# A macaron block on one core: scores of two groups in one burst, one bank for both FFNs' sums, queries and keys in one step

## The reference, cut to what matters

```python
def ffn(x):                                    # quantised weights, hidden width 2048
    gate, up = split(x @ ternary_quant(w_gate_up).T)
    return rms_norm(silu(gate) * up) @ ternary_quant(w_proj).T

def attention(x):                              # 32 heads of 16, blocks of 128 tokens
    q, k, v = x @ Wq.T, x @ Wk.T, x @ Wv.T
    # each block of 128 queries sees its own 128 keys and the 128 before them
    # (dist = query - key must lie in 0..128), none before the sequence's start
    probs = softmax(where(valid, q @ k.T / 4, lowest))
    return (probs @ v) @ Wo.T

x = x + 0.5 * ffn(layernorm(x))        # A
x = x + attention(layernorm(x))        # B
x = x + 0.5 * ffn(layernorm(x))        # C
```

## Time and profile before

| | us |
|---|---|
| three runs | 2028.21, 2030.60, 2031.13 |
| median | 2030.6 |
| the profiled execution | 2030.56 |
| its span, first to last instruction | 2028.7 |
| busy: TensorE matmul | 1919.7 |
| busy: VectorE | 1541.2 |
| busy: ScalarE | 1493.1 |

### The profile page before, as it was taken

How to read it: one execution, slowest core, us unless ns; L and a number is a source line. 1 busy time by engine, 2 the same in 40 slices (tenths; PEclk the granted TensorE clock), 3 DMA queues, 4 the chain that set the end, 5 groups by cost and what they waited for, 6 DMA issues and landing times. The chain is left out here.

```text
span 2028.7 us, 37471 instructions
## 1 busy us (share of the span) xinstructions
PE 1919.7 (95%) x12447; PEld 898.9 (44%) x12688; DVE 1541.2 (76%) x4079; ACT 1493.1 (74%) x2871; POOL 510.9 (25%) x559
## 2 busy tenths in 40 slices
PE   6678899999999999999999999999999999999887
PEld 3353344444444444444444444444444444444332
DVE  8966788777876888777777888777786788777673
ACT  6837777777776777777776777777776777768672
POOL 2012222232223222322222223222223232221100
PEclk8889999999999999999999999999999999999898
DMA  7336888788887878777896788878886788768772
GB/s 233 121 71 112 147 153 147 132 141 159 149 156 126 156 145 153 136 145 150 154 159 125 138 155 153 149 131 154 159 155 120 141 153 165 144 120 154 131 136 52
DMA packets 1031648, 287.81 MB, mean 142 GB/s; under 512 B 1016096, under 2 KB 1017120, under 8 KB 1030944
## 3 DMA queue, kind: packets, MB, share of 16 engines
q1 hardware_dynamic: 1031456, 285.41, 75.9%
HBM read 25.17 MB, written 8.39 MB: 17 GB/s over the span
## 5 line engine op out<-in xcount | busy, mean ns | idle before, releaser
L731 ACT ACTIVATE masked<-masked,exp_bias,exp_scale 128x256 f32<-128x256 f32 (+1 forms) x1024 | 503.8, 562 | 8.6
L1095 PE MATMUL ps_yy<-wp_t,ht 128*128 128x512 bf16 x1978 | 481.0, 383 | 14.4 <-DMA ht<-hh 11.7
L1049 PE MATMUL ps_gu<-wgu_t,xt_A 128*128 128x512 bf16 x1940 | 473.8, 382 | 11.2 <-DVE hid L859 2.5
L1049 PE MATMUL ps_gu<-wgu_t,xt_C 128*128 128x512 bf16 x1958 | 472.6, 379 | 5.3 <-DMA xt_C<-xh 0.5
L605 ACT ACTIVATE hh<-hid 128x512 f16<-128x512 f32 x256 | 161.0, 629 | 276.3 <-DVE hid L865 271.0
L876 DVE CUSTOM_DVE_ANT_0 masked<-ps_s,mask 128x256 f32<-128x256 f32 (+1 forms) x1024 | 337.4, 385 | 0.7 <-PE ps_s L1085 0.6
L865 DVE SCALAR_TENSOR_TENSOR hid<-ps_gu,h_scale_u,hid 128x512 f32<-128x512 f32 x252 | 188.9, 750 | 185.0 <-PE ps_gu L1049 184.7
L1095 PEld LDWEIGHTS ps_yy<-wp_t,ht 128*128 128x128 f16 x2016 | 197.9, 99 | 254.5 <-DMA ht<-hh 13.5
L1049 PEld LDWEIGHTS ps_gu<-wgu_t,xt_A 128*128 128x128 f16 x2048 | 198.6, 98 | 243.3 <-issue 6.3
L1049 PEld LDWEIGHTS ps_gu<-wgu_t,xt_C 128*128 128x128 f16 x2048 | 193.4, 98 | 222.5 <-issue 2.4
L850 DVE TENSOR_TENSOR prob<-masked,prob 128x1024 f16<-128x1024 f32 (+1 forms) x256 | 278.9, 1089 | 2.4 <-ACT prob L743 2.4
(11 more groups left out here) (148 smaller groups left out, 1892.8 us busy)
## 6 DMA issues: line engine op xcount, KB each, us to landing
stream<-in_L_attn_x_dram SPq DMA_DIRECT2D x32, 256.0 KB, 3.3
pt<-prob SPq DMA_TRANSPOSE x512, 3.2
out_dram<-stream SPq DMA_DIRECT2D x32, 256.0 KB, 2.4
prob<-in_L_ffn_w_gate_up_dram SPq DMA_DIRECT2D x4, 1024.0 KB, 5.6
ht<-hh SPq DMA_TRANSPOSE x256, 3.3
stream<-in_L_ffn_w_gate_up_dram SPq DMA_DIRECT2D x3, 1024.0 KB, 5.6
stream<-in_L_ffn_w_proj_dram SPq DMA_DIRECT2D x2, 1024.0 KB, 4.9
prob<-in_L_ffn_w_proj_dram SPq DMA_DIRECT2D x2, 1024.0 KB, 4.8
```

Source lines behind the costliest of these rows:

```text
L731: t = act.activation(p, p, ACT.Exp, bias=exp_bias[:, 4 * g + h:4 * g + h + 1], scale=exp_scale[:, 0:1])
L1049: t = pe.matmul(bank[:, :], xt[s][:, part, k, :], wgu_t[:, k, at:at + CH], start=(k == 0 and part == 0), stop=(k == KD - 1 and part == 1))
L1095: t = pe.matmul(ps_y[s][:, :], ht[:, n % HRING, i, :], wp_t[:, 4 * c + i % 4, :], start=(c == 0 and i == 0), stop=(c == NC - 1 and i == 2 ...
```

## The change

Scores are issued for two groups at once, at the end of every odd step, eight matmuls in a row. The first group goes into `ps_s` as before; the second goes into `ps_x` and `ps_m`. For that, A and C share one bank for their sums (`ps_y`), and the bank that comes free is `ps_x`. Queries and keys are both projected in step 0, the queries into `ps_m` and the keys into `ps_x`; values move to step 4 and the output projection to step 6. Each projection now waits in addition until both groups of its step are read (`d_mx`). PV stands before up. On VectorE, projections' low halves come first, the first group's maxima next, and the second group's maxima after `gated` and the low half of the probabilities; `add_ffn` stands before `hidden`; the normalisation stands after the probabilities. The output's split is in the same step as its projection.

```diff
-    Q_AT, K_AT, V_AT = 8, 9, 11
+    Q_AT, K_AT, V_AT = 8, 8, 12
-    NORM = PV + 1
-    SPLIT_O, WO_AT = NORM + 7, 23
-    LN_C, XHAT_C, SPLIT_C = 24, 25, 26
+    NORM = PV
+    SPLIT_O, WO_AT = NORM + 8, 22
+    LN_C, XHAT_C, SPLIT_C = 23, 24, 26
...
-        ps_y = {"A": ps_yy[:, 0:CH], "C": ps_yy[:, CH:2 * CH]}
+        ps_y, ps_x = ps_yy[:, 0:CH], ps_yy[:, CH:2 * CH]
+        ps_sc = ((ps_s[:, 0:CH], ps_s[:, CH:2 * CH]), (ps_x, ps_m))
...
 @@ VectorE, step_of @@
+                b, g = group_at(step, SCORES)
+                if b is not None and g % 2 == 0:
+                    masked_max(b, g)
+                b = block_at(step, SPLIT_O)
+                if b is not None:
+                    take_lo(oh[:, 1, :], o_norm[:, :], oh[:, 0, :], a_oh, b + 1, d_ol)
...
+                s, bf, c, n = gate_at(step)
+                if s:
+                    gated(s, bf, c, n)
+
+                b, g = group_at(step, PROB)
+                if b is not None:
+                    need(dve, t_pl[g % 2], 16 * (4 * b + g // 2))
+                    take_lo(prob_part(prob[:, g % 2, 1, :, :, :], b), prob_f32(b, g),
+                            prob_part(prob[:, g % 2, 0, :, :, :], b), a_ph, 8 * b + g + 1, d_pl)
+                b, g = group_at(step, SCORES)
+                if b is not None and g % 2 == 0:
+                    masked_max(b, g + 1)
+                b, g = group_at(step, NORM)
+                if b is not None and g % 2:
+                    normalise_o(b, g // 2)
...
 @@ TensorE, step_of @@
+                b, g = group_at(step + 1, SCORES)
+                if b is not None and g % 2 == 0:
+                    if step + 1 == SCORES:
+                        pe.wait_ge(a_lo, 8)
+                    need(pe, d_mx, 2 * groups_by(step, SCORES))
+                    projections_taken(step - 1)
...
+                    scores(b, g, ps_sc[0])
+                    scores(b, g + 1, ps_sc[1])
...
                 b = block_at(step, Q_AT)
                 if b is not None:
                     pe.wait_ge(t_x["B"], 16 * (b + 1))
                     need(pe, d_x2, b - 1)
                     need(pe, d_v, b)
+                    need(pe, d_mx, 2 * groups_by(step + 1, SCORES))
                     if b == 0:
                         pe.wait_ge(a_lo, 4)
-                    project(Q, xt["B"], p_q)
+                    project(Q, xt["B"], p_q, ps_m)
                 b = block_at(step, K_AT)
                 if b is not None:
-                    pe.wait_ge(a_q, b + 1)
+                    project(K, xt["B"], p_k, ps_x)
+                b = block_at(step, V_AT)
+                if b is not None:
+                    pe.wait_ge(a_k, b + 1)
                     pe.wait_ge(d_q, b + 1)
-                    project(K, xt["B"], p_k)
...
+                    need(pe, d_mx, 2 * groups_by(step + 1, SCORES))
```

More of the change, by code:

```diff
@@ L298, in macaron @@
         assert len(AT_STEP) == len(GATES) == 2 * NB * NC - NC
+        assert all(QUARTERS[n][1:3] == QUARTERS[n - n % NC][1:3] for n in range(len(QUARTERS)))
         def gate_at(step):
@@ L490, in _ @@
                     normalised_t("A", b, p_up["A"], 8 * b)
[L491 to L495, removed]
                 s, b, c = ffn_at(step)
@@ L946, in step_of, with add_output @@
             def step_of(step):
[L947 to L953, removed]
+                def add_output(b):
+                    dve.wait_ge(p_wo, b + 1)
+                    dve.scalar_tensor_tensor(out=slot(b), in0=ps_m[:, :], scalar=out_scale[:, 0:1], in1=slot(b),
+                                             op0=ALU.mult, op1=ALU.add).then_inc(d_x2, 1)
                 b = block_at(step, Q_AT + 1)
@@ L993, in step_of @@
                         attention_weight(n)
-                b = block_at(step, WO_AT + 1)
-                if b is not None and b < LAST:
-                    add_output(b)
+                b = complete("A", step, 2)
+                if b is not None:
+                    add_ffn("A", b, d_x1)
+                b = complete("C", step, 2)
+                if b is not None:
+                    add_ffn("C", b, d_x3)
                 s, bf, c = ffn_at(step)
@@ L1012, in step_of @@
                                       ALU.subtract, ALU.mult).then_inc(d_xh, 1)
-                b = block_at(step, SPLIT_O)
-                if b is not None and b < LAST:
-                    output_lo(b)
-                b = complete("A", step, 2)
-                if b is not None:
-                    add_ffn("A", b, d_x1)
-                b = complete("C", step, 2)
-                if b is not None:
-                    add_ffn("C", b, d_x3)
                 b = block_at(step, LN_B)
@@ L1069, in attention_weight, with project, scores @@
                 t.then_inc(a_tr, 1)
-            def project(m, tokens, done):
+            def project(m, tokens, done, bank):
                 for k in range(KD):
                     for n, (part, w) in enumerate(((0, wat_hi), (0, wat_lo), (1, wat_hi))):
-                        t = pe.matmul(ps_m[:, :], tokens[:, part, k, :], w[m][:, k, :], start=(k == 0 and n == 0),
+                        t = pe.matmul(bank[:, :], tokens[:, part, k, :], w[m][:, k, :], start=(k == 0 and n == 0),
                                       stop=(k == KD - 1 and n == 2))
                 t.then_inc(done, 1)
-            def scores(b, g):
+            def scores(b, g, banks):
                 at_block = b % BPS
@@ L1175, in output_projection, with projections_taken @@
                 need(pe, d_x2, b)
-                project(O, ot, p_wo)
+                need(pe, d_mx, 2 * groups_by(step + 1, SCORES))
+                project(O, ot, p_wo, ps_m)
+            def projections_taken(step):
+                for offset, done in ((Q_AT, d_q), (K_AT, d_k), (V_AT, d_v), (WO_AT, d_x2)):
+                    b = block_at(step, offset)
+                    if b is not None:
+                        pe.wait_ge(done, b + 1)
             def step_of(step):
                 if step == LAST_WO:
-                    output_projection(LAST)
+                    output_projection(LAST, step)
                 s, b, c, n = gate_at(step)
```

78 lines of the change are left out of this document (34 added, 44 removed).

## The result

The changed kernel takes 2198.2 us (2195.4 to 2208.7), 1.085 times the kernel before, interval 1.0825 to 1.0866. The forecast was 2180, in a range of 2098 to 2236. The profiled execution of after is the slowest of its four: 2208.74 us, against 2030.56 before, so the traces differ by 178 us where the medians differ by 167. All times are medians; one execution of e9 and one of the kernel before beside it took over 3930 us, nearly twice the others, and are left out.

The account below looks back on a forecast made before the run. TensorE's issue was taken to bound the steady part. Waits of 4.9 us less 0.84 gain a block, over 28 blocks, add 114 us and the clock 36 to 2030.56: 2180.6 us, range 2098 to 2236.

Parts of the forecast that it names:

- The gain: TensorE, around the scores: 0.21 us of gaps paid once for two groups, saving 0.84 us a block, 27 us in all.
- The shared bank: A's and C's sums in one bank: costs nothing, since the next block's first down comes 4.5 us later.
- Queries: Step 0: the queries' projection waits 0.95 us for VectorE's second maxima, ending at 7.08; no wait in a sequence's first block.
- Output: Step 6: the output projection waits 1.7 us; second maxima end at 7.69 and ot lands at 7.85.
- Values: Step 4: the values' projection waits 3.2 us; 2.9 in a sequence's first block, 0.7 in the block after it.
- The chain from step 2: VectorE and ScalarE, steps 2 to 4: late second maxima delay hidden, so it ends at 2.71 instead of 0.97 in step 4.
- the rival without it: No carry-over into step 4: the values wait only 1.45 us and the clock stays; 2108 us, chance 0.22.
- what is next late: Following the delay through step 4: hidden, ScalarE's copy, tanh, gated, low probabilities, then second maxima end at 9.31.
- The clock: Values after a 3.2 us wait run at half the clock, 1.7 us more in 3 of 4 blocks: 36 us.
- the rivals with the clock falling at both or at all waits: Clock also falls in step 6: 2228 us, chance 0.15; at all three waits, step 0 too: 2264 us, chance 0.05.
- The ends: Start and end of the run: both kernels wait for VectorE there anyway, so no difference taken.
- the sign: Whole kernel: slower 0.90, faster 0.07, same 0.03.

Follow-up runs that it names:

- e9: From e7, PV moved behind up in even steps, odd steps left as they were: 2043.5 us, ratio 1.0076.
- e8: From e7, the first group's scores go ahead of up and the second group's behind it, so nothing is issued together: 2084.9 us, ratio 1.0285.
- e7: From e5, on SyncE ot is issued before ht, and the high probabilities' transfer before those of q and k: 2063.8 us, ratio 1.0183.
- e10: The kernel before the change, with only A's and C's sums put in one bank: 2027.7 us, ratio 0.9996.
- e3: From the changed kernel, in steps 0, 4 and 6 VectorE does low probabilities, second maxima, then gated: 2159.0 us, ratio 1.0647.
- e1: From the changed kernel, in step 2 alone the second group's maxima go behind hidden: 2181.7 us, ratio 1.0752.
- e5: From e3, first maxima before the odd step's low hh, statistics of B and C behind gated, oh split one step earlier: 2143.7 us, ratio 1.0574.
- e11: From e9, VectorE reads ps_m first of the second group's banks and a projection waits for that half alone: 2018.3 us, ratio 0.9954.
- e2: From the changed kernel, eight gate-form matmuls with unused results stand before the values in step 4: 2212.7 us, ratio 1.0914.

## Why the prediction was right

**The gain.** Forecast 0.84 us a block, 27 in all. e8 against e7 gives 21 us. The mechanism is confirmed; the price is a little smaller. That may be because e8 gives VectorE its first group earlier, which no run separates. The shared bank, which the forecast took as free, costs nothing (e10).

**Queries.** Forecast 0.95 us of idle time in three blocks of four, none in a sequence's first. Measured 1.02 and, from TensorE's 6.13, 1.19 us later in three of four; 5.73 and no wait in the fourth.

**Output.** Forecast 1.7 in every block; measured 1.63 to 2.02 in the steady part. Both releasers that the forecast put at the same moment (7.69 and 7.85) appear in the list of waits. e3 shows that the second alone is enough to hold it: with the maxima earlier, all 32 waits are for `ot`.

**Values.** Forecast starts at 9.3, 9.3, 9.0 and 6.8; measured 6.78 in every block that follows a sequence's first, and otherwise 7.8 to 10.0. The mean over the steady part is 8.55 us against 8.6. The size is right and the cause only in part, so that the means agree so closely is partly luck. The chain from step 2 is in the trace as written, link by link, but e1 takes it away and gains 16 us, where the rival without it lay 72 us below the forecast. The step that failed is "what is next late": PV of step 4 waits 0 to 2.7 us for the low probabilities' transfer. The forecast looked at SyncE only for what changed its place there, and never followed that transfer. VectorE's lateness alone would hardly cause this wait: over 26 blocks of the steady part of after, a transfer issued at once and landing in 3.2 us would make PV wait 0.1 us on the mean, and it waits 1.0. Most of it comes from SyncE's order, which issues the low half 0.7 us or more after it is ready; in some blocks the transfer itself is slow too (5.0 us for the one that landed at 1335.29, with the load of the next tokens under way from 1328.48 to 1333.44; no run separates the two). In after this lies mostly under the values' wait; it comes out as soon as that is shortened, in e1, and it shrinks when SyncE's order is changed, in e7.

**The clock.** This term was mis-sized. Forecast: half the clock at the values in three of four blocks, 36 us. In the 27 intervals of the steady part it fell 9 times, and all stretched groups together lost some 15 us. After 2 us of idle time it went both ways. Rows of TensorE in after, first of an output projection:

```profile
1546.80 4.23 PE L1073 MATMUL ps_om<-wo,ot 128*128 128x512 f16 x12 [2.02 <-DMA ot<-oh]
```

and of a PV that waited longer, with the up and the values behind it:

```profile
1335.38 0.55 PE L1105 MATMUL ps_om<-v,pt 128*128 128x33 f16 x16 [2.48 <-DMA pt<-prob]
1335.78 3.08 PE L1048 MATMUL ps_gu<-wgu_t,xt_C 128*128 128x512 bf16 x8
1338.66 3.29 PE L1073 MATMUL ps_om<-wv,xt_B 128*128 128x512 f16 x12
```

In four blocks the clock fell already at PV. Up then took about 1 us longer, and the values came late without a wait of their own (9.93 us here). The forecast took one wait of 3.2 us; really it is broken in two by PV and up, 0.92 and 1.98 in the block shown, and mostly the clock stayed up. The Trainium skill's rule weighed in the forecast ("TensorE: Matmul & The Clock Gate", section "A second HAM failure mode: psum-queue depth-cycling") would have short frequent idle times make the clock swing. The trace does not bear that out here: in the steady part 20 waits of 1.02 us before the queries never brought it down, and of 27 waits of 1.6 to 2.0 us before the output one did. Only waits near 2 us and longer did. So the rivals with the clock falling at both or at all waits are out.

**The ends.** This is the term that put the forecast below the result. It said "I take no difference". Measured: head 6.8, first interval 6.4, last three 25.1, tail 3.0, together 41 us, where the steady rate on those four intervals is 20. The reason given was that both kernels wait for VectorE there. They do, but not equally long: in the last three intervals TensorE waits 20.4 us before and 35.9 after. Five waits at the same projections as in the steady part, only longer, make 19.7 of the latter, each with a projection at the lower clock behind it, of this form:

```profile
2048.84 4.84 PE L1073 MATMUL ps_om<-wo,ot 128*128 128x512 f16 x12 [5.09 <-DVE row_max L876]
```

The experiments agree. The last three intervals take 25 us more than before in after and 24 in e5, but 11 in e7, where only SyncE's order differs from e5; the head's 6.8 us are gone in e5. The remaining 10 us in e9 are open.

**The sum.** Steady part: 136.7 us measured. The forecast's 5.35 us a block (4.07 and 1.28 for the clock) would be 144 over the same 27. By the projections' starts the waits are about 5.1 us a block (4.91 forecast), PV outside step 4 adds 0.14, the gain takes 0.84, and the clock costs 0.4 outside the values' starts: 4.8 of 5.06, and some 0.2 is not assigned. So the clock was taken some 20 us too dear, the waits some 12 too cheap, and the ends 36 us too cheap: 41 measured, where one block's worth, 5, was in the sum for them. Together the forecast is 28 us below the profiled execution and 18 below the median. That it came so near is in part luck, since the clock's error and the two others cancel. The forecast of the sign was safer than its size: only with four further sets of edits (e5, e7, e9, e11) does the change come out ahead, by 0.5%.

## What to carry to other kernels

An instruction batched on the busiest engine saves the gaps around it (here 1%), but the engine that reads the result gets twice the work in one piece, and every wait on "all read" moves by that much: work out that reader's chain first. If a wait guards several banks, let the reader take first the bank that is needed first, and wait for that one alone (35 us here for a few lines). A transfer is only as early as the last unmet wait ahead of it in its queue, so follow the queue before moving a producer.

## What the hardware showed beyond this

- **A transfer queue is a place of its own on the path.** Making `oh` a step earlier gained nothing until its issue moved ahead of `ht` on SyncE; then, with the probabilities' transfer also moved, 80 us (e5 to e7). Each transposing transfer also occupies the issuing queue for 1.2 to 1.3 us in the rows shown.
- **After idle time near 2 us the clock went either way.** In the steady part of after, 1.98, 1.99, 2.00 (twice), 2.02 and 2.05 us were followed by half the clock; 1.99 (twice), 2.01 and 2.12 were not; and the three between 2.37 and 2.68 all were. The four runs of after range over 13 us, those of before over 3, and those of after follow the granted clock: 2208.7 us at 0.967, 2200.8 at 0.970, 2195.4 and 2195.5 at 0.974.
- **Unused matmuls hold the clock but not the time** (e2): 9 fewer projections of values at the lower clock, and 14 us slower.
